# Bringing the forward sums into the reverse passes on TensorE, with one buffer of sums

## The reference, cut to what matters

```python
src2, dst2 = concatenate([src, dst]), concatenate([dst, src])   # forward, then reverse
e2 = concatenate([e, e])
e2 = e2 / segment_sum(e2, dst2)[dst2]
# loops and edges with src == dst weigh 0
def f(y):
    return segment_sum(y[src3] * e3, dst3, num_segments=N)
k1 = f(x)
k2 = f(x + k1 / 3)
k3 = f(x + (k2 - k1 / 3))
k4 = f(x + (k1 - k2 + k3))
y = x + 0.125 * (k1 + 3 * (k2 + k3) + k4)
```

## Time and profile before

| | |
|---|---|
| time, median of 3 runs | 18223.73 us |
| lowest and highest run | 18201.41 and 18237.62 us |
| span of the profiled execution | 18199.8 us |
| instructions | 134071 |
| PE busy | 9887.9 us |
| DVE busy | 6104.5 us |
| ACT busy | 2627.5 us |
| POOL busy | 13173.8 us |

### The profile page before, as it was taken

One profiled execution on the slowest core, in us unless ns is written; L12 is line 12 of the kernel. 1 busy time (PEld: TensorE's weight loads), 2 busy tenths in 40 slices (PEclk: granted clock), 3 DMA queues, 4 the chain that ended last, 5 costly groups with the idle time before them and its releaser, 6 DMA issues.

```text
span 18199.8 us, 134071 instructions
## 1 busy us (share of the span) xinstructions
PE 9887.9 (54%) x41175; PEld 6958.0 (38%) x41175; DVE 6104.5 (34%) x10064; ACT 2627.5 (14%) x4408; POOL 13173.8 (72%) x13148
## 2 busy tenths in 40 slices
PE   6503545555558864455554555545555555549755
PEld 2303434443423353344443444334443344434443
DVE  8601111111168875222222222222222222236422
ACT  0000111111137632011111111111111111110011
POOL 5877777777777788777776777777777777760377
PEclk8655565555589987555555555555555555559755
DMA  1101121121123332111112211122122221217422
GB/s 36 22 3 49 52 51 52 52 52 52 49 64 106 105 82 61 50 53 52 53 53 55 53 53 53 53 56 53 52 53 54 54 53 53 53 55 295 183 53 57
DMA packets 591326, 1154.17 MB, mean 63 GB/s; under 512 B 256151, under 2 KB 323359, under 8 KB 564758
## 3 DMA queue, kind: packets, MB, share of 16 engines
q0 software_dynamic: 420480, 761.05, 17.1%
q1 hardware_dynamic: 166659, 383.98, 5.9%
q10 hardware_dynamic: 3600, 1.51, 0.0%
HBM read 831.58 MB, written 312.20 MB: 63 GB/s over the span
## 4 chain that ended last, share of the span: by engine, by line
POOL 71%; issue 23%; PE 4%; DVE 1%; DMA 1%; ACT 0%; POOLq 0%; SPq 0%; ACTq 0%; DVEq 0%
POOL rows L466 55%; POOL list_r L450 6%; POOL list_f L450 6%; POOL rows L477 4%; PE ps L1250 4%; PE ps L1089 0%; PE ps L1143 0%; DMA rows<-table,rows_F 0%; DVE work L1030 0%; DMA work<-in_edge_attr_4x_dram 0%; DVE work L1024 0%; DMA rows<-table,rows_R 0%; DVE work L1033 0%; PE ps L1160 0%; DMA table<-work 0%
## 5 line engine op out<-in xcount | busy, mean ns | idle before, releaser
L1143 PE MATMUL ps<-rows,onehot 128*128 128x128 f32 (+1 forms) x22880 | 5411.7, 411 | 6220.9 <-DVE rows L811 4163.4
L1143 PEld LDWEIGHTS ps<-rows,onehot 128*128 128x128 f32 x22880 | 4666.5, 301 | 7483.3 <-issue 4832.3
L466 POOL DMA_INDIRECT rows<-table,rows_F x6160 | 5921.1, 961 | 1993.7 <-issue 1873.3
L466 POOL DMA_INDIRECT rows<-table,rows_R x3520 | 3347.7, 951 | 1080.0 <-issue 1071.5
L520 ACT COPY work<-ps 128x1188 f32 x1430 | 1641.8, 1148 | 13682.6 <-PE ps L1149 13675.4
L797 DVE TENSOR_TENSOR onehot<-iota,list_F 128x512 f32<-128x512 f32 x1980 | 1285.4, 690 | 3112.1 <-ACT work L520 3112.1
L1132 PE MATMUL ps<-naught 128*128 128x396 bf16 x4290 | 1601.2, 508 | 1208.4 <-issue 1208.4
L466 POOL DMA_INDIRECT rows<-rel_table,rows_F x880 | 834.8, 949 | 1015.2 <-DMA rel_table<-list_R 747.3
L811 DVE TENSOR_TENSOR rows<-rows,list_F 128x512 f32<-128x512 f32 x880 | 616.4, 700 | 2450.2 <-DMA rows<-table,rows_F 2450.2
L811 DVE TENSOR_TENSOR rows<-rows,list_R 128x512 f32<-128x512 f32 x880 | 615.3, 699 | 2433.7 <-DMA rows<-table,rows_R 2433.7
L450 POOL DMA_INDIRECT list_r<-list_R,rows_R x850 | 1151.2, 1354 | 259.2 <-issue 259.2
(11 more groups left out here) (206 smaller groups left out, 5231.1 us busy)
## 6 DMA issues: line engine op xcount, KB each, us to landing
rel_table<-list_R SPq DMA_DIRECT2D x196, 1024.0 KB, 3.8
rows<-table,rows_F POOLq DMA_INDIRECT x6160, 2.5
gat_rows<-rows SPq DMA_DIRECT2D x220, 264.0 KB, 2.1
rows<-gat_rows SPq DMA_DIRECT2D x220, 264.0 KB
rows<-table,rows_R POOLq DMA_INDIRECT x3520, 2.5
rows<-gat_table,rows_F POOLq DMA_INDIRECT x880, 2.6
rows<-rel_table,rows_F POOLq DMA_INDIRECT x880, 2.5
list_f<-list_F,work POOLq DMA_INDIRECT x850
```

Of the source, the lines that this page charges most:

```text
L466: pool.indirect_dma_start(out=rows[:, t % UNROLL, 0:FEAT], out_offset=None, in_=from_table, in_offset=bass.IndirectOffsetOnAxis(ap=rows_of ...
L1143: ins = mm(into, onehot[:, s, :], rows[:, s, 0:width], start=False, stop=True, skip_group_check=True)
```

## The change

In the reverse passes PE no longer brings in only the window's first block. With three identity products of 396 columns, one for each bank, it brings in what the sums hold for all nine slots, which in a reverse pass are the forward sums (and, for the first block, forward and begun reverse sum). So the store writes forward plus reverse, R needs no buffer of its own, and the add of `ACC_R` on DVE is gone. The sums' buffer is not cleared at the start of R. The words behind the last block, which the nine slots of the last windows reach, are cleared once before layer 0. F, and the other passes, keep the one product.

```diff
--- before.py
+++ after.py
@@ -122,9 +122,8 @@
         H = sb("H", [P, BLOCKS, FEAT])
         work = sb("work", [P, 2 * SUM_WORDS])
         K = work[:, 0:BLOCKS * FEAT].rearrange("p (b f) -> p b f", f=FEAT)
-        sums_flat = {"R": work[:, 0:SUM_WORDS], "F": work[:, SUM_WORDS:]}
-        SUM_OF = {key: flat.rearrange("p (b f) -> p b f", f=AUX)[:, 0:BLOCKS, :] for key, flat in sums_flat.items()}
-        ACC, ACC_R = SUM_OF["F"], SUM_OF["R"]
+        sums_flat = work[:, SUM_WORDS:]
+        ACC = sums_flat.rearrange("p (b f) -> p b f", f=AUX)[:, 0:BLOCKS, :]
         lists = {"F": sb("list_F", [P, TILES, W]), "R": sb("list_R", [P, TILES, W])}
         rows_of_list = {"F": sb("rows_F", [P, TILES], I32), "R": sb("rows_R", [P, TILES], I32)}
         slot_of = {"F": sb("slot_F", [1, TILES], I32), "R": sb("slot_R", [1, TILES], I32)}
@@ -306,6 +305,10 @@
         def windows_before(name):
             return WINDOWS * SUMS.index(name)
 
+        def adds(name):
+
+            return name.endswith(" R")
+
         def quad_of_rows(q):
             return rows[:, q % QRING * QUAD:(q % QRING + 1) * QUAD, :].rearrange("p t f -> p (t f)")
 
@@ -517,7 +520,7 @@
             act.sem_inc(shares_exp, 1)
             def store_window(key, w, m0, firsts):
                 act.wait_ge(window_summed, m0 + w + 1)
-                nc.scalar.copy(sums_flat[key][:, bass.ds(firsts[w % 10], SLOTS * AUX)].rearrange("p (k f) -> p k f", k=SLOT_BANKS),
+                nc.scalar.copy(sums_flat[:, bass.ds(firsts[w % 10], SLOTS * AUX)].rearrange("p (k f) -> p k f", k=SLOT_BANKS),
                                half_of[w % 2][:, :, 0:SLOTS * AUX // SLOT_BANKS]).then_inc(window_stored, 1)
 
             def store_windows(name):
@@ -812,7 +815,10 @@
 
             def sums_begin(name):
 
-                v.memset(SUM_OF[name[-1]][:, 0, :], 0.0).then_inc(sums_clear, 1)
+                if adds(name):
+                    dve.sem_inc(sums_clear, 1)
+                else:
+                    v.memset(ACC[:, 0, :], 0.0).then_inc(sums_clear, 1)
                 members_of_window(name, 0)
 
             def sums_end(name):
@@ -1009,6 +1015,7 @@
             dve.wait_ge(table_ready, parts_through("rk0"))
             st(v.tensor_tensor(X[:, :, :], X[:, :, :], H[:, :, :], ALU.add))
 
+            st(v.memset(sums_flat[:, BLOCKS * AUX:], 0.0))
             for k in range(4):
                 if k:
                     table_at(dve, f"rk{k}")
@@ -1018,10 +1025,8 @@
                         name_rows("R", 0)
                     attr = lists[key][:, :, 3:3 + HEADS]
                     block_sums(f"rk{k} {key}", weights=attr, aux=attr if k == 0 else None)
-                n = AUX if k == 0 else FEAT
                 for lo, hi in THIRDS:
                     A, count = ACC[:, lo:hi, 0:FEAT], hi - lo
-                    st(v.tensor_tensor(ACC[:, lo:hi, 0:n], ACC[:, lo:hi, 0:n], ACC_R[:, lo:hi, 0:n], ALU.add))
                     if k == 0:
                         st(v.tensor_scalar(REC[:, lo:hi, :], ACC[:, lo:hi, FEAT:AUX], TINY, None, ALU.max))
                         st(v.reciprocal(REC[:, lo:hi, :], REC[:, lo:hi, :]))
@@ -1146,8 +1151,16 @@
 
                     if m0 + w:
                         pe.wait_ge(window_stored, m0 + w)
-                    mm(half[:, 0:width], ident[:, :], sums_flat[key][:, bass.ds(offsets["firsts"][w % 2], width)],
-                       start=False, stop=True, skip_group_check=True).then_inc(window_summed, 1)
+                    first = offsets["firsts"][w % 2]
+                    if adds(name):
+                        cleared = SLOTS * AUX // SLOT_BANKS
+                        for k in range(SLOT_BANKS):
+                            ins = mm(half_of[w % 2][:, k, 0:cleared], ident[:, :], sums_flat[:, bass.ds(first + k * cleared, cleared)],
+                                     start=False, stop=True, skip_group_check=True)
+                    else:
+                        ins = mm(half[:, 0:width], ident[:, :], sums_flat[:, bass.ds(first, width)],
+                                 start=False, stop=True, skip_group_check=True)
+                    ins.then_inc(window_summed, 1)
 
             def block_sums(name, width=FEAT):
                 offsets = {}
```

## The result

The changed kernel takes 18291.06 us (median of five, 18281.05 to 18294.48), against 18223.73 us before: the ratio is 1.0035, with a 95% interval from 1.0024 to 1.0047. I had forecast a median of 18206.7 us, with a chance of 0.82 for a time from 18178 to 18250 us. The profiled execution has a time of 18281.05 us and spans 18279.1 us, 79.3 us more than the 18199.8 us of before. (Before's profiled execution took 22 us less than its own median, after's 10 us less than its own, which is why the two medians are only 67 us apart.)

The account below looks back on a forecast made before the run. POOL's gathers bound the passes, the PE, ACT and DVE chain the time between. Adds -28.6 us plus tails 11.6 us gave -17.0 us: 18223.7 to 18206.7 us, range 18178 to 18250 us (chance 0.82).

Parts of the forecast that it names:

- What bounds the kernel: Inside a pass POOL's gathers, 1.245 us each; between passes the chain of PE, ACT and DVE steps.
- the first rival: Inside R: PE at 1.2 GHz needs over 9.96 us a window and becomes the bound; +71 us, chance 0.08.
- The work of a window: In one window of R, PE needs 8.8 to 9.3 us at 1.2 GHz, within POOL's 9.96 us.
- The adds: Between passes: removing the twelve adds of the reverse sums takes 28.6 us off the chain.
- The tails: Last window of each R, without gathers to hide under: longer identities add 2.9 us, four times, 11.6 us.
- Small terms: Clear at the start, register additions and instruction fetches for PE: taken at 0, fetches at most 4 us.
- the last transfer: End of R: the table's last third still starts on an empty queue; cost taken 0, at most 1.5 us.
- The standstill on the table: POOL's wait between passes falls: layer 0 from 36.0 to about 31.6 us, the three from 102.3 to some 90.
- The clock in R: PE's granted clock in the reverse passes, 0.55 before, would be over 0.6.
- The step that failed: Inside R, DVE's masks start 1.4 us later behind the later store; cost of the change inside the pass: 0.
- the 1110 that I had named as a sign of being wrong: Reverse passes were to be as long as forward ones; R over 1110 us would show the prediction wrong.
- The third rival: DVE's gain given back by R gathers that PE lengthens (10 ns, 35 us) or by transfers; 18242 us, chance 0.10.

Follow-up runs that it names:

- set 6: Load behind again (0.9995), and the kernel before with a 392-word DVE clear ahead of R's masks (1.0063); the kernel before took 18237.02 us.
- masks early: The changed kernel with R's masks on DVE waiting for PE's sums instead of ACT's store: 18175.06 us, 0.9991 of the kernel before.
- load behind: The kernel before with three more fp32 products of 396 columns behind each identity of R: 18230.78 us, 0.9995.
- the sets of 20.1 to 20.3 ms: The first four sets of follow-up runs, where the kernel before took 20100.09, 20268.86, 20317.72 and 20099.50 us.
- set 2: Changed kernel (1.0008), masks early (0.9999), load behind (1.0005), kernel before with a clear ahead of R's masks (1.0012); the kernel before took 20268.86 us.

## Why the prediction was wrong, point by point

- **What bounds the kernel** was right: POOL inside a pass, the chain between passes. PE never became the bound (waits of POOL on PE 3.7 us, 4.0 before), so the first rival didn't come. The work of a window fitted as summed: six identity records took 3.80 us at the lower clock and 2.16 us at the upper, where I had 3.96 and 1.98.
- **The adds**: predicted 28.6 us, measured 28.6. In layer 1 the time from the store's start to DVE's first step of the next layer fell from 27.93 to 20.82 us, in layer 0 from 30.66 to 23.33.
- **The tails**: predicted 11.6 us (2.4 to 14), measured 8.4. From the last quad's begin to the store it is 3.28, 5.79, 4.91 and 4.97 us, where it was 2.6 to 2.7: extras of 0.6, 3.2, 2.3 and 2.4 us. The largest, in layer 1, answering:

```profile
11879.51 2.07 PE L1148 MATMUL ps<-rows,onehot 128*128 128x128 f32 x8 [3.96 <-DVE rows L814]
11881.37 3.80 PE L1158 MATMUL ps<-work,ident 128*128 x6
11885.30 1.15 ACT L523 COPY work<-ps 128x1188 f32 x1 [12.02 <-PE ps L1158]
11886.48 2.63 DVE L1035 SCALAR_TENSOR_TENSOR work<-work,REC 128x544 f32<-128x544 f32 x4 [7.11 <-ACT work L523]
```

- **Small terms**: the clear at the start took 0.94 us behind idle, the instruction queue brought 17 more packets in the run (361, from 344), and the last transfer still starts free. All at nothing, as said. The standstill on the table at three places is 86.7 us, where I had some 90; in layer 0 it is 29.2 us, where I had 31.6, since PE's clock was up in that tail.
- **The clock in R** rose to 0.81, as I had it (over 0.6).
- **The step that failed** is the one on the masks inside the pass: they "would start 1.4 us later", and nobody is waiting for them, "so inside the pass I cost the change at 0". It asked who waits for a delayed step. It did not ask what that step holds up while it runs. The masks and the scalings stood harmlessly because both followed the landing of POOL's own data; with the store later, it became what the masks waited for last in 284 of 440 windows, and that broke it. The price is 84 us in R, of which 10.6 belong to the 3 ns of the usual gather (below), and the forecast of R passes as long as F's went with it: R took 1123 to 1128 us, over the 1110 that I had named as a sign of being wrong.
- **The third rival** had the outcome (gathers in R lengthened, gain given back) at a chance of 0.10, but not the cause or the size: I put it on PE's reads and fetches, with 10 ns a gather and 35 us. It was 24 ns a gather, nearly all of it by DVE's steps; PE's reads cost nothing (951 ns with them, set 6). My argument against it, that at the same load F and R have the same, was no argument: the offsets of DVE's steps were alike too. A gather of 1.45 us stood in the window that I read, and I passed over it.
- The median of 18291.06 us lies beyond my upper end of 18250. With the gathers as they were, the change does what the sum said: masks early is at 0.9991 (0.9982 to 1.0001), 15 us under before, against the 17 forecast. It is the fastest of all kernels here, though its interval does not quite leave out no gain.

What stays open: the usual gather takes 944 ns in some loads of a kernel and 947 in others (the changed kernel has shown 947, 947, 944 and 944, load behind 944, 947 and 944). The scatters of the lists move with it, from 1187 to 1190 ns. Over the 13140 gathers and scatters that is 30 to 40 us, it is no property of a kernel, and what sets it was not found. In the first comparison it accounts for 10.6 us of the 84 in R and more than covers the 14.5 outside. Open is also what delays the word of PE's sums in the sets of 20.1 to 20.3 ms.

## What to carry to other kernels

Where POOL's gathers bound a kernel, a step of DVE with two inputs in SBUF is never free just because nobody waits for it: count the gathers that begin while it runs, here some 0.56 us minus the offset for each. Release such steps by something on POOL's own beat (the landing of its data), and be wary of an edit that makes them follow another engine. And when a bounding engine's waits have not changed, compare the mean duration of its instructions, and then their spread, before asking anything else.

## What the runs showed of the hardware

- A gather begun up to 0.55 us into a two-input step of 0.69 us on DVE lasts up to 1438 ns in the mean instead of 944, the less the later it begins. In the first 40 ns almost none is held up (4 of 3289), and one that began ahead of the step not at all. Steps without SBUF input hold up nothing: 440 gathers begun during clears, -0.1 us. The Trainium skill, page "SBUF — State Buffer", section "Who interferes with whom", has a rule for this: a DVE instruction with two SBUF inputs contends with a GpSimd instruction that reads SBUF, whichever comes first holding the shared port until it is done, while one with at most one such input does not. The runs agree that the two-input steps contend and the clears don't. They don't agree on the whole of "until it is done": the hold ends 0.56 us into a step of 0.69 us, and DVE's steps are not held up by a gather begun before them (0.67 to 0.70 us in the mean, against 0.72 to 0.73 for those begun between gathers). The same section infers that `tensor_tensor` doesn't hold up the making of descriptors; here gathers issued from POOL were held up by it for up to 0.49 us in the mean, and the measurement decides. Which part of a gather is held up, its read of the row numbers or another, no run here tells. I had not drawn on this rule for the prediction.
- PE's load is free for POOL: 410 us more PE busy time in the run (10297.3 us, set 6) changed no gather.
- A chip can be in a condition in which POOL stands still 40 to 54 times a pass for 2.8 to 3.9 us in the mean, and the kernel takes 20.1 to 20.3 ms instead of 18.2. In the trace of the changed kernel in set 2 the data had landed and was scaled each time, and POOL went on only 13.9 us (median) after PE's records of the sum that it waited for. One chip showed both, in sets 2 and 6. What brings it about was not found.
